# Layer A's channel-major rows: from a second input with spread statistics to token-major fp16 parts turned by DMA transposes

## What is computed

```python
def _layernorm(x, axis=-1, eps=1e-05):
    m = jnp.mean(x, axis=axis, keepdims=True)
    v = jnp.var(x, axis=axis, keepdims=True)
    return (x - m) / jnp.sqrt(v + eps)
...
        q = (x @ Wq.T).reshape(b, n, NUM_HEADS, HEAD)
        k = (x @ Wk.T).reshape(b, n, NUM_HEADS, HEAD)
        v = (x @ Wv.T + bv).reshape(b, n, NUM_HEADS, HEAD)
        bias = (spatial_encoding + edge_encoding)[:, None]
        scores = jnp.einsum('bqhd,bkhd->bhqk', q, k) * scale + bias
...
        p = jax.nn.softmax(scores, axis=-1)
        p = jnp.nan_to_num(p)
        out = jnp.einsum('bhqk,bkhd->bqhd', p, v).reshape(b, n, h)
        return out @ Wo.T + bo
...
    x = x + _L0_gnn_ref(_layernorm(x, axis=-1), adj, adj, L0_gnn_Wq, L0_gnn_Wk, L0_gnn_Wv, L0_gnn_bv, L0_gnn_Wo, L0_gnn_bo)
    x = x + _L0_ffn_ref(_layernorm(x, axis=-1), L0_ffn_Wqk, L0_ffn_bqk, L0_ffn_Wv, L0_ffn_bv, L0_ffn_conv_w, L0_ffn_conv_b, L0_ffn_glob, L0_ffn_pos_bias, L0_ffn_Wg1, L0_ffn_bg1, L0_ffn_Wg2, L0_ffn_bg2, L0_ffn_Wp, L0_ffn_bp)
    return x
```

## Time and profile before

| | us |
|---|---|
| median of 3 runs | 2218.86 |
| range of the runs | 2217.16 to 2220.27 |
| span of the profiled execution, first to last instruction | 2214.1 |

### The profile page before, as it was taken

One profiled execution on the slowest core, in us unless ns is written; L12 is line 12 of the kernel. 1 busy time (PEld: TensorE's weight loads), 2 busy tenths in 40 slices (PEclk: granted clock), 3 DMA queues, 4 the chain that ended last, 5 costly groups with the idle time before them and its releaser, 6 DMA issues.

```text
span 2214.1 us, 51113 instructions
## 1 busy us (share of the span) xinstructions
PE 2167.0 (98%) x16581; PEld 1388.2 (63%) x16581; DVE 1959.1 (88%) x7242; ACT 1490.3 (67%) x5298; POOL 1198.7 (54%) x1521
## 2 busy tenths in 40 slices
PE   5899999999999999999999999999999999999988
PEld 3566666666666666666666666666666666666655
DVE  6889998889988899988899988899988899888984
ACT  4667766677666676666676666677666776666763
POOL 2755565555565545565545665555655555655452
PEclk9999999999999999999999999999999999999999
DMA  5332333332333332333322333322333323333200
GB/s 178 77 93 54 80 90 98 92 84 55 88 87 101 92 77 58 92 87 92 100 69 59 100 87 92 99 52 75 94 94 92 83 59 86 87 101 92 47 27 29
DMA packets 182105, 182.62 MB, mean 82 GB/s; under 512 B 48977, under 2 KB 173521, under 8 KB 181841
## 3 DMA queue, kind: packets, MB, share of 16 engines
q1 hardware_dynamic: 179648, 178.07, 31.1%
q10 hardware_dynamic: 2192, 1.29, 0.2%
HBM read 78.50 MB, written 25.29 MB: 47 GB/s over the span
## 4 chain that ended last, share of the span: by engine, by line
PE 93%; DVE 3%; SPq 1%; ACT 1%; DMA 1%; issue 1%; POOL 0%; DVEq 0%
PE B_bank L546 33%; PE A_bank L546 32%; PE A_bank L626 7%; PE A_bank L638 4%; PE B_bank L620 4%; PE B_bank L645 4%; PE A_bank L613 4%; PE B_bank L630 2%; PE B_bank L589 2%; DVE raw_score L1001 1%; SPq L521 1%; DMA x1res<-in_wqk 1%; DVE smax L1007 0%; DVE V L990 0%; ACT S L755 0%
## 5 line engine op out<-in xcount | busy, mean ns | idle before, releaser
L1147 POOL TENSOR_TENSOR S<-S,rowf 128x512 f32<-128x512 f32 x384 | 414.9, 1108 | 459.9 <-DVE rowf L1026 457.1
L748 ACT ACTIVATE S<-raw_score,smin 128x128 f32<-128x128 f32 x1536 | 595.0, 392 | 94.6 <-DVE smin L1001 94.6
L1001 DVE CUSTOM_DVE_ANT_0 raw_score<-A_bank,adj,s_unit 128x128 f32<-128x128 f32 x1536 | 433.1, 344 | 6.5 <-PE A_bank L613 3.4
L1152 POOL TENSOR_TENSOR S<-S,row2f 128x384 f32<-128x384 f32 x128 | 105.8, 826 | 450.2 <-DVE row2f L1034 447.2
L748 ACT ACTIVATION_READ_ACCUMULATOR S<-raw_score,smin 128x1 f32 x1536 | 293.4, 191 | 0.0
L626 PE MATMUL A_bank<-ident,S 128*128 128x128 f32 x1536 | 218.7, 275 | 5.9 <-POOL S L1147 5.2
L1007 DVE TENSOR_REDUCE smax<-raw_score 128x12 f32<-128x1536 f32 x128 | 222.7, 1740 | 0.0
L762 ACT ACTIVATE PT<-A_bank 128x512 f32<-128x512 f32 x384 | 210.0, 590 | 7.6 <-PE A_bank L626 6.9
L626 PEld LDWEIGHTS A_bank<-ident,S 128*128 128x128 f32 x1536 | 176.5, 141 | 33.2 <-issue 10.4
L713 ACT ACTIVATE b_hT_hi<-B_bank 128x512 f16<-128x512 f32 x96 | 53.2, 588 | 191.1 <-PE B_bank L589 191.1
L762 ACT ACTIVATE PT<-B_bank 128x384 f32<-128x384 f32 x128 | 62.8, 491 | 158.9 <-PE B_bank L630 158.9
(11 more groups left out here) (196 smaller groups left out, 6330.0 us busy)
## 6 DMA issues: line engine op xcount, KB each, us to landing
xin<-in_x SPq DMA_DIRECT2D x32, 768.0 KB, 5.0
Qs<-q_hi SPq DMA_DIRECT2D x256, 96.0 KB, 2.2
out<-x1res SPq DMA_DIRECT2D x128, 192.0 KB, 2.1
Ks<-k_hi SPq DMA_DIRECT2D x252, 96.0 KB, 3.2
xt<-in_xT SPq DMA_DIRECT2D x30, 768.0 KB, 4.2
stat_wide<-stat_rows SPq DMA_DIRECT2D x30, 512.0 KB, 4.4
Qs<-q_lo SPq DMA_DIRECT2D x128, 96.0 KB, 2.2
Ks<-k_lo SPq DMA_DIRECT2D x126, 96.0 KB, 2.9
```

Of the source, the lines that this page charges most:

```text
L748: ins = nc.scalar.activation(S[b % 2][:, h, :], raw_score[:, h, :], ACT.Exp, bias=smin[b % 2][:, h:h + 1], scale=-1.0, accum_out=ssum[b % ...
L1001: ins = nc.vector.tensor_tensor_reduce(raw_score[:, h, :], src[:, j * T:(j + 1) * T], adj2[:, b, :], s_unit[:], 3.0e38, ALU.add, ALU.min, ...
L1147: nc.gpsimd.tensor_tensor(S[b % 2][:, hs, :], S[b % 2][:, hs, :], rowf[b % 2][:, hs].unsqueeze(2).broadcast_to([P, HPC, T]), ALU.mult).the ...
L1152: nc.gpsimd.tensor_tensor(S2[b % 2][:], S2[b % 2][:], row2f[b % 2][:].unsqueeze(2).broadcast_to([P, NE, T]), ALU.mult).then_inc(normed2, 1)
```

## The change

The input xT, its load, the round trip of the statistics through DRAM, and the steps A.hx, A.hm, A.stat, A.rows and A.xT go, and so do the transposes on TensorE in groups 0 and 1. In all groups GpSimd now makes the rows of h1 token-major, one batch a step (A.h1), into two buffers in turn; ScalarE and VectorE split each batch into fp16 parts, still token-major (`h1_parts`, 128 x 768 a batch: 384 high and 384 low); and SyncE turns each batch by one DMA transpose into `h1T` (six blocks of 128 channels x 128 tokens). hT has four steps now, one a batch, of 128 x 384. GpSimd writes row b of h1 when VectorE is done with row b - 2. TensorE waits for all four transfers of the group before the first matmul of A.qk.0.

```diff
-        xt = sb("xt", [P, KC, GB * T])
-        h1 = xt[:].rearrange("p c n -> p (c n)").rearrange("p (b n) -> p b n", b=GB)
+        h1 = sb("h1", [P, 2, C])
+        h1_parts = sb("h1_parts", [P, GB, 2, C], F16)
+        h1T = sb("h1T", [P, GB, 2 * KC, T], F16)
...
-                if (stage, kind) == ("A", "xT") and not last:
...
-                    sp.dma_start(xt[:], xT[following(g)]).then_inc(xT_loaded, 16)
-                if (stage, kind) == ("A", "stat"):
...
-                if (stage, kind) == ("A", "rows"):
...
+                if (stage, kind) == ("A", "hT"):
+
+                    wait_evacuated(sp, step, g)
+                    if b == 0 and not g == 0:
+                        wait_products(sp, ("A", "v", GB - 1, 0), before(g))
+                        wait_products(sp, ("A", "qk", 2 * KC - 1, 0), before(g))
+                    sp.dma_start_transpose(h1T[:, b, :, :],
+                                           h1_parts[:, b, :, :].rearrange("p n c -> p (n c)")).then_inc(h1_turned, 16)
...
+                if A and kind == "qk" and b == 0:
+                    pe.wait_ge(h1_turned, count(g, 16 * GB, 16 * GB))
+
+                def columns(c):
+                    return [h1T[:, :, n + c, :] for n in (0, KC)] if A else [h[:, c, :] for h in (hT_hi, hT_lo)]
+
+                def tokens(c):
+                    return [h1T[:, b, n + c, :] for n in (0, KC)] if A else [h[:, c, tok(b)] for h in (hT_hi, hT_lo)]
...
+                elif kind == "hT" and A:
+
+                    act.wait_ge(h1_ready, count(g, GB, b + 1))
+                    if b == 0 and not g == 0:
+                        act.wait_ge(h1_turned, count(g, 16 * GB, 0))
+                    nc.scalar.activation(h1_parts[:, b, 0, :], h1[:, b % 2, :], ACT.Copy, scale=H_SCALE)\
                         .then_inc(hi_ready["ahead"], 1)
...
-                elif kind == "hm":
-                    dve.wait_ge(centred, count(g - TURNED, KC, b + 1))
-                    nc.vector.tensor_tensor(xt[:, b, :], xt[:, b, :], stat_wide[:, 1, :], ALU.mult).then_inc(hx_ready, 1)
...
+                    rows_in, hi, lo = ((h1[:, b % 2, :], h1_parts[:, b, 0, :], h1_parts[:, b, 1, :]) if A else
+                                       (src[:, :], hT_hi[:, b, :], hT_lo[:, b, :]))
+                    nc.vector.scalar_tensor_tensor(out=lo, in0=rows_in, scalar=H_SCALE, in1=hi,
+                                                   op0=ALU.mult, op1=ALU.subtract)\
...
+            def normed_rows1(g, b):
                 pool.wait_ge(rstd1_done, count(g, 1, 1))
+                if b >= 2:
+                    wait_evacuated(pool, ("A", "hT", b - 2, 0), g)
+                elif not g == 0:
+                    wait_evacuated(pool, ("A", "hT", b + 2, 0), before(g))
+                nc.gpsimd.tensor_scalar(h1[:, b % 2, :], xin[g % 2][:, b, :], stat[g % 2][:, 0, b:b + 1],
+                                        stat[g % 2][:, 1, b:b + 1], ALU.add, ALU.mult).then_inc(h1_ready, 1)
...
     "pool": """
-        A.res.0 A.ln1 A.res.1 B.res.0 B.res.1 A.norm.0 A.res.2 A.res.3 A.norm.1 A.hx.0 A.hx.1 A.hx.2 A.norm.2
-        B.norm.0 B.norm.1 B.res.2 A.norm.3 B.norm.2 B.norm.3 A.ln2.0 B.res.3 A.ln2.1 A.ln2.2 A.ln2.3 A.adj
+        A.res.0 A.ln1 A.res.1 B.res.0 B.res.1 A.norm.0 A.res.2 A.res.3 A.norm.1 A.h1.0 A.h1.1 A.h1.2 A.h1.3
+        A.norm.2 B.norm.0 B.norm.1 B.res.2 A.norm.3 B.norm.2 B.norm.3 A.ln2.0 B.res.3 A.ln2.1 A.ln2.2 A.ln2.3
+        A.adj
```

More of the change, by code:

```diff
@@ L88 @@
     "pe": """
[L89 to L93, removed]
@@ L99 @@
[L99 to L103, removed]
@@ L104 @@
-        A.turn.3.1@0 A.turn.3.2@0 A.mix.3@0
+        A.hT.0@0 W.hi.0@0 A.hT.1@0 W.hi.1@0 A.hT.2@0 A.hT.3@0 W.sum.5@0 W.sum.4@0 A.qk.0@0 A.qk.1@0 W.sum.3@0
+        A.qk.2@0 A.qk.3@0 W.sum.6@0 A.qk.4@0 A.qk.5@0 W.hi.2@0 W.stack.1@0 A.score.0.0@0 A.score.0.1@0
+        A.score.0.2@0 W.hi.3@0 A.hT.0@1 A.score.1.0@0 W.hi.4@0 A.score.1.1@0 A.score.1.2@0 A.hT.1@1 A.turn.0.0@0
+        W.hi.5@0 A.turn.0.1@0 A.hT.2@1 A.hT.3@1 A.score.2.0@0 A.turn.0.2@0 W.hi.6@0 A.score.2.1@0 A.mix.0@0
+        A.qk.0@1 A.turn.1.0@0 A.qk.1@1 A.turn.1.1@0 W.hi.7@0 A.turn.1.2@0 A.score.2.2@0 A.qk.2@1 A.score.3.0@0
@@ L206, with crossed @@
 }
-def turned(step, g):
-    return step[:2] == ("A", "hT") and g >= TURNED
+def crossed(step):
+    return step[:2] == ("A", "hT")
 def parse(word):
@@ L222, in ahead @@
 def ahead(step):
-    return step[0] == "A" and step[1] in ("hT", "qk", "stack", "xT", "stat", "rows", "hx", "hm")
+    return step[0] == "A" and step[1] in ("hT", "qk", "stack", "h1")
 def whole_program(engine):
@@ L243 @@
 LATE = 4
-TURNED = 2
 def evac_engine(step):
@@ L596, in do @@
                     mm = three_pass(dst[:, :], lambda c: [w[:, c, m * P:(m + 1) * P] for w in W],
[L597 removed]
+                                    columns, wait_hT)
                 elif kind == "v":
@@ L691, in do @@
                 A = stage == "A"
-                src = bank_of(step, g) if kind in EVAC and not turned(step, g) else None
+                src = bank_of(step, g) if kind in EVAC and not crossed(step) else None
                 if kind == "hi":
@@ L1117, in _ @@
             statistics1(0)
-            normed_rows1(0)
+            for b in range(GB):
+                normed_rows1(0, b)
             pool.wait_ge(bo_loaded, 16)
```

140 lines of the change are left out of this document (44 added, 96 removed).

## The result

| | before | after |
|---|---|---|
| median of 4 runs, us | 2218.01 | 2288.95 |
| range of the runs | 2216.13 to 2220.27 | 2284.72 to 2291.85 |
| span of the profiled execution | 2214.1 | 2289.4 |
| its own time | | 2291.18 |

The change makes the kernel slower: the ratio is 1.032, with an interval of 1.0305 to 1.0335. The forecast was 2275, its range 2226 to 2620. (The four runs before are the three of the earlier table and one more.)

A forecast was written before the change was run, and what follows sets the result against it. The prediction took TensorE's instructions to bound the kernel: 2214.1 span + 50 (waits for transposes) + 6 (start) = 2270 us, and with the median 4.8 us above the span, 2275 us; range 2226 to 2620.

The forecast's parts named there:

- What bounds the kernel: Steady loop: TensorE, busy 98% of the span, sets the turn; work removed from GpSimd, VectorE and DMA is worth nothing itself.
- The chain: Steps from h1 rows through splits ahead of A.qk.0: low parts end at 1060.4, 1063.1, 1063.6 and 1064.9.
- The two buffers: h1 in the steady turn: GpSimd writes row 3 only after VectorE's A.hT.1, so A.hT.3 is late, at 1064.9.
- The price of a transpose: SyncE's queue: 1.3 us for 192 KB, landing 1.56 us later, taken from SBUF-to-SBUF stack transfers (0.64 us per 96 KB).
- The steady wait: TensorE at A.qk.0 waits 1.65 us a turn for the last transpose, 30 turns, 50 us.
- rival 1: Transposes hold the queue longer: 3 us each, 7 us wait a turn plus lost clock, 2481; up to 3070; chance 0.30.
- The start: Groups 0 and 1: late transposes behind weight loads against 24 removed TensorE transposes; +6 us, bounds -5 to +10.
- ScalarE's 0.7 us: ScalarE's fourth A.hT passes 0.7 us to score exponentials and A.turn.1.2; TensorE's wait covers it, else up to 0.7 a turn.
- 4.8 us between span and median: Final sum: the runs' median 2218.86 stands 4.8 us above the profiled span, carried from 2270 to 2275.
- Rivals: Alternative outcomes: longer queue hold (0.30), like one plain transfer, about 2230 (0.17), chain hidden, 2213 to 2223 (0.08).
- neither end: Transpose price bounds: low, like a plain store or stack transfer, landing after 2.1 to 2.2 us; high, 7.9 us a transfer.

The follow-up runs named there:

- experiment 5: Changed kernel with four h1 buffers and the whole chain (h1 rows, high and low splits) earlier in the steady turn: 2237.8 us, ratio 1.0084.
- experiment 7: Changed kernel with four h1 buffers, early chain, group 1's steps regrouped in the first lists, and one transpose per two batches: 2226.72 us, ratio 1.0035.
- experiment 1: Changed kernel with four h1 buffers instead of two, order and transposes kept: 2286.7 us, ratio 1.0307.
- experiment 4: Changed kernel with each batch turned by two transposes of 384 columns (96 KB) instead of one of 768: 2462.43 us, ratio 1.1098.
- experiment 8: The kernel with one transpose per two batches, with group 0's rows split earlier, ahead of the weights' work on ScalarE and VectorE: 2228.13 us, ratio 1.0044.
- experiment 6: Changed kernel with four h1 buffers and group 1's h1 rows, splits and transposes grouped earlier in the first lists: 2280.25 us, ratio 1.0282.
- experiment 3: Changed kernel without transposes behind group 0, TensorE waiting for VectorE's fourth low part instead (output not the reference's): 2240.15 us, ratio 1.0097.
- experiment 2: Changed kernel with VectorE's maxima A.smax.2 (1.74 us) moved behind A.hT.3, still two buffers: 2251.1 us, ratio 1.0145.

## Why the prediction was right, and where it was wrong

- **What bounds the kernel:** right. VectorE lost 3.6 us of work a turn (60.66 busy before, 57.07 after), and the time did not fall. With the wait gone (experiments 5 and 7) the turn is 66.91 us, TensorE's work.
- **The chain:** right within 0.3 us. TensorE stood ready at 1066.96 before and at 1108.79 after, 41.83 later; with that added, the forecast's low parts are at 1102.2, 1104.9, 1105.4 and 1106.7, measured 1102.21, 1104.81, 1105.27 and 1106.95.
- **The two buffers:** named as what makes A.hT.3 late, which they do, and left out of the wait, which experiment 1 bears out.
- **The price of a transpose:** the right number for a wrong reason. I took 1.3 us of queue and 1.56 us from there to the landing; measured are 1.29 and 1.6. But 1.3 was twice the 0.64 us of a 96 KB stack transfer, by bytes, and experiments 4 and 7 show that the hold does not follow the bytes: 1.26 and 1.29 us for 96 and 192 KB, and 1.48 to 1.81 for 384. That the number fitted at 192 KB was luck. By bytes, halves would have held 0.65 us each and cost nothing; they cost 173 us.
- **The steady wait:** 1.65 us a turn forecast, 1.57 to 1.65 in most turns. 50 us were forecast, 57.8 measured by the forecast's count; 7 us of that are the longer waits and the clock, which the forecast put at nothing below rival 1's long pauses. It drew on one pause of 2.22 us at full clock; here the clock fell behind 2.04, 2.17 and 2.20 us and did not behind 2.64.
- **The start** is the step that failed: +6 us, bounds -5 to +10, measured +18.5, or +16.9 by the forecast's count. In group 0 the mechanism was named (transposes behind the weight loads), but they were priced like those of a steady turn; behind the loads the first landed 6.1 us after its issue, and the last 2.5 us later than the forecast's upper end, at 29.35. (The last low part came at 24.28, not 22.6; experiment 8 shows that this did not set the end.) For group 1 I assumed the wait of a steady turn, without reading its lists: rows 2 and 3 of h1 stand there behind A.norm.0 and A.norm.1 of group 0, and SyncE's transposes behind A.res. That made the wait 10.8 us (experiment 6). Group 0 weighs more: A.qk.0 of group 2 stands at 148.07, 147.64 with four buffers, 145.29 with group 1's lists, 142.38 with the pairs and the early chain, 133.07 with group 0 on TensorE, and 129.53 before; so group 0's transposes made 9.3 of the 18.5 us, and the lists of group 1 alone 2.35.
- **ScalarE's 0.7 us** that TensorE's wait would cover, "up to 0.7 us a turn" without it: right; experiment 3 uncovers 0.32.
- **4.8 us between span and median:** not a property of the kernel. In the changed kernel's runs the own time is 1.8 us above the span; the other 3 were the place of that one execution among its runs. The error is small and was to the forecast's good. Against the profiled execution's own 2291.18, the forecast of 2275 is the sum of a start 11 us too small, a loop 8 us too small and these 3 us the other way.
- **Rivals:** the transposes' price lay at neither end. Of the two pages cited, the Trainium skill's "Advanced Engine Details and Errata", section "X-Bar Transpose (TRN2)", has 350 GB/s or more; here 96 KB more made the landing 0.44 us later (2.43 to 2.87), some 220 GB/s, on top of the fixed part; while the transposes of the turn above run, the DMA view of 1105 to 1111 us has the engines at 0.9 or more of their time and 181 to 227 GB/s. "VectorE: DVE Perf Modes", section "The three transpose paths", has 1309 ns for one block; here three blocks and six hold 1.26 and 1.29 us, so it is near what a whole transfer holds the queue for, and six in a row do not take six times that.

Still open: why some transposes land 0.6 to 1.4 us late. The traces show what they coincide with. In groups 2 to 31 of the changed kernel, ten groups have a transfer of instructions (8 or 16 KB) that starts while their transposes are in flight, and six of these have a transpose that lands over 0.3 us later than the median or holds the queue for over 1.64 us; of the other 20 groups one has. The four long waits (groups 5, 17, 20 and 29) are all among the ten. In experiments 1, 2, 4, 5, 6 and 7 it is 28 groups of 48 with such a transfer, and 2 of 132 without (the limits there 0.3 and 0.35 us above the run's median). That the one makes the other late is not shown, since no run moved these transfers.

## What to carry to other kernels

Price a small DMA by its place in its queue before its bytes: count how many stand behind the last thing that makes them wait, and where the hold is mostly per transfer, as here from 96 to 384 KB, send fewer and larger ones, or start the chain earlier. A wait moves off the path by reordering other engines' lists (one move of a 1.74 us reduction gave 38 us here), and what it had covered appears next. The first groups run by lists of their own; read them step by step, on every queue, as carefully as the steady turn.

## What the runs showed of the hardware

- A DMA transpose held SyncE's queue for 1.26 us at three blocks of 128 x 128 fp16, 1.29 at six and 1.62 at twelve in the median (1.48 with none just ahead of it, 1.81 right behind another); it landed 2.4, 2.9 and 4.0 us after its issue. The Trainium skill's page "DMA: Bandwidth & Descriptors", section "Rules for kernel authors", says to merge many small transfers into a large one; the traces agree, by 173 us between eight transposes a group and four in the same order (2462.43 and 2288.95).
- Behind loads that fill the DMA engines a transpose held the queue for up to 7.4 us and landed up to 10.4 us after its issue (experiment 8, 388 GB/s at 20 to 22 us).
- Reading h1T in four runs of 128 columns costs the matmuls nothing: 379 ns each, as for one run of 512.
